# Softmax attention: the four transfers of the maxima's row move from SP's queue to ScalarE's

## The reference

```python
def _L0_xattn_ref(x, c, Wq, bq, Wk, bk, Wv, bv, Wo, bo):   # 8 heads of 8 channels, 256 positions
    q = split_heads(_proj(x, Wq, bq))
    k = split_heads(_proj(c, Wk, bk))
    v = split_heads(_proj(c, Wv, bv))
    q = _apply_rotary(q_emb, q)
    k = _apply_rotary(k_emb, k)
    scores = jnp.einsum('bhtc,bhsc->bhts', q, k) / math.sqrt(K_CH)
    p_attn = jax.nn.softmax(scores, axis=-1)
    out = jnp.einsum('bhts,bhsc->bhtc', p_attn, v)
    return _proj(out.transpose(0, 1, 3, 2).reshape(b, N_HEADS * K_CH, t_t), Wo, bo)

x = x + jnp.tanh(g_xattn[0]) * _L0_xattn_ref(_layernorm(x, axis=-1), ctx_2048, ...)
x = x + jnp.tanh(g_ffn[0]) * _L0_ffn_ref(_layernorm(x, axis=-1), ...)      # 8 experts, top 2
...
```

## Time and profile before

| what | value |
|---|---|
| median of 3 runs | 2698.87 us |
| lowest and highest run | 2694.81 and 2713.35 us |
| span of the profiled execution | 2704.4 us |
| granted TensorE clock, mean of the span | 0.898 |
| the stage's steady part, start of `both(1, 0)` to `both(31, 0)` | from 79 to 650 us of the span |

### The profile page before, as it was taken

The page is one execution under the profiler, slowest core; times in us unless marked ns, Lnnn a source line. Parts: engine busy times, 40 slices in busy tenths (PEclk is TensorE's granted clock), DMA queues, the critical chain, the costliest instruction groups (busy, mean ns, idle before and its releaser), DMA issues. The chain is left out here.

```text
span 2704.4 us, 60407 instructions
## 1 busy us (share of the span) xinstructions
PE 2266.0 (84%) x20880; PEld 1712.8 (63%) x20880; DVE 1858.8 (69%) x3965; ACT 1160.7 (43%) x2509; POOL 1108.1 (41%) x1111
## 2 busy tenths in 40 slices
PE   5898888988677689995698998999978598999990
PEld 3555555554565567774477777777766577887770
DVE  4798787773546667765687788788787365445754
ACT  2676666565433323332344444444333263333330
POOL 3454544475144500000354454454387600224626
PEclk9798887675789899998899999999999899999995
DMA  5445554452358531101323323323234472446754
GB/s 120 115 122 139 118 128 114 98 138 90 117 167 263 180 129 58 60 25 48 80 59 82 86 59 81 84 57 83 72 97 117 131 244 75 135 139 181 236 159 142
DMA packets 249859, 313.10 MB, mean 116 GB/s; under 512 B 45152, under 2 KB 202848, under 8 KB 249056
## 3 DMA queue, kind: packets, MB, share of 16 engines
q1 hardware_dynamic: 188592, 219.11, 29.3%
q0 software_dynamic: 26624, 58.79, 7.9%
q10 hardware_dynamic: 34352, 31.34, 3.4%
HBM read 122.40 MB, written 102.24 MB: 83 GB/s over the span
## 5 line engine op out<-in xcount | busy, mean ns | idle before, releaser
L730 DVE TENSOR_REDUCE soft_top<-soft_pa 128x2 fp32r<-128x512 f32 x512 | 328.7, 684 | 121.1 <-PE soft_pa L810 118.4
L2083 POOL TENSOR_TENSOR ca_qk<-ca_qk,ca_q_swap 128x512 f32<-128x512 f32 x160 | 249.4, 1559 | 365.2 <-DVE ca_q_swap L2261 364.8
L625 ACT ACTIVATE soft_prob<-soft_pb 128x512 f32<-128x512 f32 x512 | 285.4, 594 | 212.2 <-PE soft_pb L803 209.7
L803 PE MATMUL soft_pb<-soft_rep 25*128 25x256 f32 x1024 | 211.7, 384 | 59.7 <-DMA soft_rep<-soft_peak 26.8
L803 PEld LDWEIGHTS soft_pb<-soft_rep 25*128 25x128 f32 x1024 | 138.2, 229 | 184.8 <-issue 84.2
L1415 PE MATMUL moe_pgu<-moe_w_hi,moe_xt_hi 128*128 x472 | 196.0, 415 | 39.7 <-DVE moe_xt_lo L1332 29.8
L810 PE MATMUL soft_pa<-soft_rep 24*128 24x256 f32 x1024 | 220.6, 390 | 6.0 <-DVE soft_top L730 3.5
L1434 PE MATMUL moe_py<-moe_w_d,moe_at 128*128 x788 | 217.8, 392 | 1.5 <-issue 0.8
L1337 DVE TENSOR_TENSOR moe_act_f<-moe_silu,moe_pgu 128x256 f32<-128x256 f32 (+1 forms) x236 | 88.5, 375 | 154.5 <-ACT moe_silu L1252 151.4
L2352 PE MATMUL ca_py<-ca_w_hi,ca_ot_hi 128*128 128x256 f32 x512 | 154.3, 301 | 36.6 <-DVE ca_ot_lo L2282 36.3
L1252 ACT ACTIVATE moe_silu<-moe_pgu 128x256 f32<-128x256 f32 (+1 forms) x236 | 82.5, 349 | 232.4 <-PE moe_pgu L1415 232.3
(11 more groups left out here) (377 smaller groups left out, 6440.2 us busy)
## 6 DMA issues: line engine op xcount, KB each, us to landing
ca_q_swap<-ca_q_f SPq DMA_DIRECT2D x640, 64.0 KB
moe_xs<-moe_rows SPq DMA_DIRECT2D x236, 128.0 KB, 2.1
soft_rep<-soft_parts SPq DMA_DIRECT2D x378, 64.0 KB
moe_rows<-soft_blank SPq DMA_DIRECT2D x27, 768.0 KB
moe_ys_rows<-moe_ys ACTq DMA_DIRECT2D x134, 128.0 KB, 1.7
moe_ys<-moe_ys ACTq DMA_DIRECT2D x102, 128.0 KB, 2.4
moe_xd<-scratch SPq DMA_DIRECT2D x64, 128.0 KB, 2.5
ca_vs<-ca_v SPq DMA_DIRECT2D x32, 256.0 KB, 3.9
```

What stands on the lines that cost most here:

```text
L625: act.activation(prob[:, k % 4, h, :], p_b[:, 2 * T * h:2 * T * (h + 1)], ACT.Exp).then_inc(prob_ready, 1)
L730: dve.tensor_reduce(heads[:, j, :, g], p_a[:, 2 * T * h:2 * T * (h + 1)].rearrange("p (c s) -> p c s", c=HALF), AX, ALU.max).then_inc(a_do ...
L803: mm = pe.matmul(p_b[:, out], rep[of, i % 4, g, at:at + PART], rep[of, i % 4, g, 0:T], start=True, stop=True)
L2083: pool.tensor_tensor(qk[:, u % 2, m, :], qk[:, u % 2, m, :], q_swap[:, p % 2, :], ALU.add).then_inc(qk_ready, 1)
```

## The change

The four transfers are taken out of SP's list and put into ScalarE's, between `exp(i, 6)` and `keep(i, 1)`, with SP's wait on `peak_ready` and one more wait, on `b_ready`, that the slot of `rep` is free. Their number, shapes and semaphores stay as they were. SP no longer waits for `peak`.

```diff
@@ SP @@
-                    n = i + 1
-                    if live(n):
-                        sp.wait_ge(peak_ready, n + 1)
-                        for j in range(4):
-                            at = 32 * j + SPLIT
-                            sp.dma_start(rep[at:at + 1, n % 4, :, 0:T].bitcast(fp32), peak[4 * j:4 * j + 4, n % 2, :].bitcast(fp32)
-                                         ).then_inc(peak_in[n % 2], 16)
                     if i == 8:
                         held.load(sp)
@@ ScalarE @@
                     exp(i, 6)
+                    n = i + 1
+                    if live(n):
+                        act.wait_ge(peak_ready, n + 1)
+                        past(act, b_ready, 2 * PAIRS * (n - 3))
+                        for j in range(4):
+                            at = 32 * j + SPLIT
+                            act.dma_start(rep[at:at + 1, n % 4, :, 0:T].bitcast(fp32), peak[4 * j:4 * j + 4, n % 2, :].bitcast(fp32)
+                                          ).then_inc(peak_in[n % 2], 16)
                     keep(i, 1)
                     exp(i, 7)
```

## The result

The kernel after took **2730.86 us** (median of four runs, 2726.21 to 2740.60), the kernel before 2697.98 beside it (2694.81 to 2713.35): ratio **1.011, interval 1.0081 to 1.014**, some 30 us slower. The direction is the forecast's and the time lies in its range, but the loss is about twice the 16 us that were predicted. The profiled execution spans 2724.4 us, 20.0 more than that of before; 18.7 of these lie before `both(31, 0)`, which starts at 669.11 instead of 650.40. It is the shortest of the four, so what follows accounts for some 20 of the 30 us.

What follows compares the result with a forecast made beforehand. TensorE was nearest its limit, with transfers and ScalarE's list meeting at tile boundaries. 17.0 + 7.7 + 0.2 - 4.5 = +20.4 us, less 4 caught up, gave +16 on 2698.9: 2715 us, range 2688 to 2748.

Steps and rivals of the forecast that it cites:

- What ScalarE pays: In ScalarE's list at tile boundaries: four issues delay `exp(i, 7)` and `y` by 1.75 us; boundaries cost 17.0 + 7.7 + 0.2.
- tile 10's gain: At tile 10, where SP issued late and TensorE stopped 4.94 us, ScalarE's issuing would gain 4.5 us.
- the 4 caught up: Later in the round, where TensorE waits for VectorE, 4 us of the delay would be recovered, turning +20.4 into +16.
- I count 0: On SP's side, the zeros leaving some 4 us earlier, into GpSimd's eight transfers, would cost nothing: 0 us.
- up to 1 us a round at the five boundaries with loads: VectorE's reciprocal waiting for GpSimd's transfers would cost this much if TensorE's own boundary delay did not cover it.
- the wait for `soft_peak` falls by tile 10's five: Sign in the profile after: TensorE's wait for the row falls by five us, staying at tiles 4, 12 and 20.
- The four long stops: TensorE's stops on transfers at tiles 4, 10, 12, 20: tile 10 gains 4.5 us, the others no gain, no loss.
- The transfers pass the loads: Rival: on ScalarE's otherwise empty queue 4 KB transfers overtake the loads, some 5 us lower: +11, 2710 us; chance 0.12.
- Issues are cheap on ScalarE: Rival: four issues take 1.5 us, so `exp(i, 7)` shifts 0.7 instead of 1.75: -5, 2694 us; chance 0.09.
- The issues wait for the end of `exp(i, 6)`: Rival: in ScalarE's list issues start 1 us later, unhidden, costing +27; chance 0.30 together with the clock rival.
- The clock falls: Rival: longer TensorE stops at six of eleven boundaries lower its clock: +42, 2741 us; chance 0.30 together with unhidden issues.
- Off the path: Rival: the boundary delay is caught up in the round and tile 10's stop won: 2699 us; chance 0.06.

Runs made afterwards that it cites:

- run 1: Kernel after, plus a wait of SP so that weights and the store of zeros leave once the row of `peak` has landed: ratio 1.0049.
- run 5: Kernel after, SP waiting for the row's landing before loads and zeros, and round 8's weights spread over eight rounds: ratio 1.0028.
- run 4: Kernel before, SP still issuing the row, with loads moved behind it and round 8's weights spread over rounds 8 to 15: ratio 0.9925.
- run 2: Kernel before, SP still issuing the row, with only the store of zeros moved ahead of the four issues: ratio 1.0057.
- run 10: The kernel of run 4 with the store of zeros moved ahead of SP's four row transfers: ratio 0.9970.
- run 3: Kernel before, plus four same-shaped transfers issued by ScalarE at the change's place into an unread tile; SP keeps the real four: ratio 1.0101.
- run 6: The kernel of run 5 with the row in one transfer of 16 rows of 1 KB, issued by ScalarE: ratio 0.9916.
- run 8: Kernel after with one edit, the row in one transfer issued by ScalarE, zeros and loads still ahead: ratio 0.9994.
- run 7: The kernel of run 4 with the row in one transfer of 16 rows of 1 KB, issued by SP: ratio 0.9900.

## Why the prediction was right in direction and short by half

**What ScalarE pays: right.** Start, length, the 1.5 us of idle list and the shift of `exp(i, 7)` (2.9 us behind `exp(i, 6)`) are in the profile as worked out. The size holds as well: the forecast's +16 was made of ScalarE's list less tile 10's gain, and run 1, which has these two beside SP's added wait, measured +13 (7 to 19). The forecast's 24.9 for the list alone, 20.9 with the 4 caught up, stands against 28 (20 to 36) in run 5 against run 4, where, unlike in the forecast, the boundaries of tiles 4, 12 and 20 have only short stops (0.8 to 1.6 us) to hide it in. The 4 us that were to be caught up within the round can't be told apart in these runs.

**What SP and the others get: the step that failed is "I count 0".** The text had seen that the zeros leave some 4 us earlier, and it weighed them against GpSimd's eight transfers alone. It did not weigh them against the row of `peak` itself, which lands late at the twelve boundaries where they now leave close to it. Measured: 15 us when only the zeros move (run 2), 12 in the cleared queue (run 10), 16 when they are put back and the `fill_rows` with them (run 1). The forecast had named a price without cover, "up to 1 us a round at the five boundaries with loads", but for VectorE's wait. TensorE waits for the row with no cover at all, and at ordinary boundaries like tile 13 as well.

The stated sign, "the wait for `soft_peak` falls by tile 10's five", failed with it. Tile 10 gained as forecast, 4.94 to 0.41, but the sum grew by 21.7.

**Luck.** That the time lies in the stated range is in part luck. 2731 falls into the band that was kept for a lower clock or for unhidden issues (2727 to 2755). The issues were hidden as forecast, the clock accounts for a small part at most (see the rivals below), and the cause that was left out, the zeros, had no rival of its own.

**The four long stops: half right.** Tile 10 gained; tiles 4 and 20 kept their stops, 4.38 us instead of 2.56 at the former and 4.34 instead of 4.22 at the latter. Tile 12 had only 0.39, its second load having left 6.3 us ahead of the row instead of 2.0, but tile 8, which had stopped for 1.93, stopped for 4.75, with the zeros 0.3 us ahead. One reading was wrong: at tile 20 SP had been late too, since its loads held the first issue until 430.38, 1.1 us after `peak` was evicted.

**The rivals.** *The transfers pass the loads*: rejected; on ScalarE's queue, which carries nothing else here, 4 KB transfers still landed 4.8 us behind their issue at tile 4 (137.54 against 132.75 as the end of the last issue). A queue of its own was no quick passage, as the prediction had argued from GpSimd's wait. The Trainium skill ("DMA: Bandwidth & Descriptors", section "Queues, rings and completion order") says that each DMA engine goes round robin between the queues that have work for it, packet by packet; in which order packets went no run here shows. The Trainium skill says on the same page, section "Issuing engines are not separate DMA queues", that the transfers of all issuing engines run on the same 16 DMA engines and interleave there, and the 4.8 us agree with that. *Issues are cheap on ScalarE*: rejected, 580 ns in the median, 2.42 us for four. *The issues wait for the end of `exp(i, 6)`*: rejected, they started 0.10 us behind its start at tile 13 and 0.66 at most elsewhere. *The clock falls*: not the main cause. In the steady part of the profiled executions it is 0.79 after 0.78, means over stretches at 1.2 and at 2.4 GHz. Over the whole span, though, the four timed executions of after were granted 0.886 to 0.891, those of before in the experiments 0.896 in the mean, and the longest kernels had the lowest clock (run 3 0.889, run 6 0.907, in the mean). Among the executions of before, 0.01 less went with some 5.6 us more, so by estimate 4 or 5 of the 30 us may go with the clock. Whether the clock made the time longer or the stops drew the clock down was not tested. *Off the path*: rejected by runs 3 and 5.

**What stays open.** Run 1 against after splits the 30 us into 13 and 16. But ScalarE's price alone (28), the zeros (12 to 16) and tile 10's gain (-4.5) add up to 36 to 40. That they meet at the same boundaries, where only the later one counts, would explain the excess but is argued; run 8 shows only that they aren't independent, and how the overlap divides is within the intervals and was not settled. Nor was it shown in which part of the way, the engines' queues or the memory, the zeros hold up the row.

## What to carry to other kernels

When an instruction that waits is taken out of a list, ask what stood behind it in that list and now goes early, and set that against the transfer you are trying to speed up, first of all. A list that is full can hide an issue only as long as the work handed out just before it: one issue of 0.55 us went under an exponential for nothing, four of 2.42 cost 28 us. So make one transfer of four before choosing the engine: with that, the loads put behind the row and the weights spread, the kernel ran at 0.990 of before (run 7), and on the other engine at 0.992 (run 6).

## What the runs showed of the hardware that was not expected

- A transfer of 16 rows of 1 KB took no longer to issue (543 ns in the median) than one of 4 rows (580): here the price was per transfer, not per row.
- Beside four issues of SP that read the same rows, an issue of the same shape took ScalarE 676 ns in the median instead of 580 (run 3). Ten issues of the kernel after that ran beside other issues of SP took 580 like the rest, so issuing at the same time is not enough; the cause is open.
- Behind a store of 768 KB that left on another queue 2.15 us ahead, 4 KB transfers landed about 1.9 us later (3.05 behind the last issue at tile 13, 1.16 before the change); behind one that left 7.1 us ahead they landed as before (1.17, tile 14).
